# Two mixture-of-experts layers: blocks of 256 rows become units of 128, and the second layer goes by pairs of experts

## What is computed

```python
def _L0_ffn_ref(x, Wg, W1, b1, W2, b2):
    gate_logits = xs @ Wg
    weights, sel = jax.lax.top_k(gate_logits, TOP_K)
    weights = jax.nn.softmax(weights.astype(jnp.float32), axis=1).astype(x.dtype)
    h = jax.nn.relu(jnp.einsum('td,edf->etf', xs, W1) + b1[:, None, :])
    out_e = jnp.einsum('etf,efd->etd', h, W2) + b2[:, None, :]
    picked = out_e[sel, tok[:, None]]
    out = jnp.einsum('tk,tkd->td', weights, picked)
...
x = x + _L0_attn_a_ref(_layernorm(x, axis=-1), ...)
x = x + _L0_ffn_ref(_layernorm(x, axis=-1), L0_ffn_Wg, L0_ffn_W1, L0_ffn_b1, L0_ffn_W2, L0_ffn_b2)
x = x + _L0_attn_b_ref(_layernorm(x, axis=-1), ...)
x = x + _L0_ffn_ref(_layernorm(x, axis=-1), L0_ffn_Wg, L0_ffn_W1, L0_ffn_b1, L0_ffn_W2, L0_ffn_b2)
```

## Time and profile before

| | us |
|---|---|
| median of 3 runs | 2342.39 (2342.32 to 2342.47) |
| the profiled execution | 2342.5 |
| its span | 2340.8 |
| scan | 0 to 695 |
| ffn1: groups, routing, one-hots, block loop | 710.0, 758.5, 780.3, 838.8 to 1090.0 |
| attention | 1090 to 1757 |
| ffn2: one-hots, block loop, gather | 1850, 1908, 2157 to 2341 |

### The profile page before, as it was taken

How to read it: one execution, slowest core, us unless ns; L and a number is a source line. 1 busy time by engine, 2 the same in 40 slices (tenths; PEclk the granted TensorE clock), 3 DMA queues, 4 the chain that set the end, 5 groups by cost and what they waited for, 6 DMA issues and landing times. The chain is left out here.

```text
span 2340.8 us, 52167 instructions
## 1 busy us (share of the span) xinstructions
PE 1654.0 (71%) x16780; PEld 1352.2 (58%) x16780; DVE 1857.7 (79%) x4943; ACT 1471.0 (63%) x3849; POOL 1342.9 (57%) x1496
## 2 busy tenths in 40 slices
PE   4676675766657369995689999999986459998000
PEld 2444454454546158884488888888875338887000
DVE  6999999999978957776689999999975867776221
ACT  5666676766743647774388888888883457776000
POOL 3545555555540045554399999999971035553774
PEclk8778787777865679998699999999995579999555
DMA  1000001010034013333122222222214013333232
GB/s 29 14 14 22 20 14 28 14 27 14 19 104 140 1 48 81 81 80 58 39 57 57 57 59 59 59 57 57 57 28 129 23 27 81 81 81 67 74 80 57
DMA packets 188967, 122.59 MB, mean 52 GB/s; under 512 B 24320, under 2 KB 177824, under 8 KB 188704
## 3 DMA queue, kind: packets, MB, share of 16 engines
q1 hardware_dynamic: 154016, 75.18, 11.6%
q0 software_dynamic: 17408, 35.69, 6.9%
q10 hardware_dynamic: 17280, 8.40, 1.2%
HBM read 66.22 MB, written 44.04 MB: 47 GB/s over the span
## 5 line engine op out<-in xcount | busy, mean ns | idle before, releaser
L1044 POOL DMA_INDIRECT ffn_xs<-normed,ffn_tokeni x288 | 273.1, 948 | 460.1 <-DVE posi L1420 260.7
L1877 POOL TENSOR_TENSOR att_pl<-att_p,att_ph 128x384 f16<-128x384 f32 x512 | 455.3, 918 | 56.3 <-ACT att_ph L2098 48.6
L323 POOL TENSOR_TENSOR sq<-states,qS 128x256 f32<-128x256 f32 x256 | 250.9, 980 | 304.3 <-DVE states L733 303.3
L543 ACT ACTIVATE decayed<-states,alpha 128x64 f32<-128x64 f32 x1024 | 272.3, 336 | 177.6 <-DVE states L733 175.7
L379 PE MATMUL bank<-sq,ident 128*128 128x128 f32 x1024 | 249.9, 415 | 93.4 <-POOL sq L323 93.4
L2206 DVE TENSOR_REDUCE att_mx<-bank 128x3 f32<-128x384 f32 x512 | 279.9, 552 | 41.0 <-PE bank L1934 36.8
L1251 ACT ACTIVATE ffn_h<-bank,b_cols 128x256 f32<-128x256 f32 x576 | 226.4, 475 | 127.7 <-PE bank L1139 117.4
L379 PEld LDWEIGHTS bank<-sq,ident 128*128 128x128 f32 x1024 | 220.0, 240 | 128.9 <-POOL sq L323 100.7
L2095 ACT ACTIVATE att_p<-bank 128x384 f32<-128x384 f32 x512 | 252.2, 493 | 58.9 <-PE bank L1971 55.5
L2098 ACT ACTIVATE att_ph<-bank 128x384 f16<-128x384 f32 x512 | 253.0, 494 | 0.0
L1152 PE MATMUL bank<-w_h,ffn_hh 128*128 x1152 | 225.6, 223 | 14.9 <-DVE ffn_hl L1439 4.5
(11 more groups left out here) (336 smaller groups left out, 5085.5 us busy)
## 6 DMA issues: line engine op xcount, KB each, us to landing
slots<-ffn_ys SPq DMA_DIRECT2D x144, 128.0 KB
ffn_x_all<-x SPq DMA_DIRECT2D x16, 512.0 KB, 4.8
normed<-ffn_xn ACTq DMA_DIRECT2D x32, 256.0 KB, 2.3
att_qz<-att_qp SPq DMA_DIRECT2D x256, 32.0 KB
ffn_xs<-normed,ffn_tokeni POOLq DMA_INDIRECT x288
xin<-in_x SPq DMA_DIRECT2D x64, 64.0 KB, 2.0
xres<-in_x SPq DMA_DIRECT2D x64, 64.0 KB, 2.0
x<-x SPq DMA_DIRECT2D x64, 64.0 KB, 1.8
```

The costliest lines, as they stand in the source:

```text
L323: nc.gpsimd.tensor_tensor(sq[:, t, :].rearrange("p (h i j) -> p h i j", h=HL, i=D), states[:, t, :].rearrange("p (h i j) -> p h i j", h=HL ...
L543: ins = nc.scalar.activation(decayed[:, 64 * h:64 * h + 64], states[:, (t - 1) % TC, 64 * h:64 * h + 64], ACT.Copy, scale=alpha[p][:, t, h ...
L1044: pool.indirect_dma_start(xs[j % AHEAD][:, r, :], None, A["normed"], bass.IndirectOffsetOnAxis(ap=tokeni[:, BR * j + r:BR * j + r + 1], ax ...
L1877: nc.gpsimd.tensor_tensor(pl[:, h % RP, :], p32[:, h % RP, :], ph[:, h % RP, :], ALU.subtract).then_inc(low_done, 1)
```

## The change

The list of tokens is made in units of 128 rows (P) in place of blocks of 256, and `Layout` says how: ONE, for ffn1, has 8 groups and both choices (135 units); TWO, for ffn2, has 28 groups, one for each pair of experts, and each token once (91 blocks, each worked through by both of its experts: 182 units).

The normed rows are stored as two 16-bit halves; `turn` is two 16-bit matmuls (L1175) of halves already split. The first bias becomes row 127 of W1 (row 127 itself is subtracted from the rest; the normed rows sum to zero, and their last column is replaced by 1). W1 is therefore loaded as 127 rows (L814) and the bias as one (L815), and `last_row` (L837, 127 rows) is a copy of row 127 for all partitions, loaded between the first and the second part of x. The low parts of the weights, and the subtraction, go to GpSimd. ReLU goes from PSUM straight to the 16-bit high half; DVE forms the low half from PSUM.

In ffn2 a fetched row carries halves, x and both gates (1032 bytes, from `table`); DVE adds the first expert's result to x and then the second's, and GpSimd writes the finished 128 rows to `out` with one indirect transfer for each block (L1105). The gather stage is gone. The Python loops are unrolled.

```diff
-BS = 256
-BR = BS // P
-NB = 2 * NT // BR + NX
-NS = NB * BS
...
+XB = 8
+XH = 3
+HB = 4
+YB = 4
...
+class Layout:
+    def __init__(self, groups, choices):
+        self.groups, self.choices = groups, choices
+        self.blocks = (choices * B * T + groups * (P - 1)) // P
+        self.per = 3 - choices
+        self.units = self.blocks * self.per
+        self.listed = -(-self.units // AHEAD) * AHEAD
+ONE = Layout(NX, 2)
+TWO = Layout(PAIRS, 1)
+NS = ONE.blocks * P
...
+        w1 = self.A["W1"].rearrange("e d f -> d e f")
+        sp.dma_start(self.w[0][0:P - 1, :, :], w1[0:P - 1]).then_inc(self.w_in[0], 16)
+        sp.dma_start(self.w[0][P - 1:P, :, :], self.A["b1"].rearrange("(o e) f -> o e f", o=1)).then_inc(self.w_in[0], 16)
...
+        sp.wait_ge(self.cleared, 1)
+        sp.dma_start(self.last_row[0:P - 1, :, :], A["W1"][:, P - 1, :].partition_broadcast(P - 1)).then_inc(self.last_in, 16)
         sp.dma_start(X.b2[:, :, :].rearrange("p e d -> p (e d)"),
...
+                     A["b2"].rearrange("e d -> (e d)").partition_broadcast(P)).then_inc(self.b2_in, 16)
...
+    def subtract_last(self, pool, e):
+        if e == 0:
+            pool.wait_ge(self.raw_in[0], 32)
+            pool.wait_ge(self.last_in, 16)
+        self.nc.gpsimd.tensor_tensor(self.raw[0][:, e, :], self.raw[0][:, e, :], self.last_row[:, e, :],
+                                     ALU.subtract).then_inc(self.less, 1)
...
+    def high(self, act, n):
+        k, e = (1, n) if n < NX else (0, n - NX)
+        if n == 0:
+            act.wait_ge(self.raw_in[1], 16)
+        if k == 0:
+            act.wait_ge(self.less, e + 1)
+        scale = 2.0 ** (SPLIT, DSPLIT)[k]
+        a = self.nc.scalar.activation
+        a(self.parts(k, e)[0], self.raw[k][:, e, :], ACT.Copy, scale=scale).then_inc(self.w_high, 1)
+        act.wait_ge(self.w_high, n + 1)
+        a(self.raw[k][:, e, :], self.raw[k][:, e, :], ACT.Copy, scale=scale).then_inc(self.w_full, 1)
+    def low(self, pool, n):
+        k, e = (1, n) if n < NX else (0, n - NX)
+        pool.wait_ge(self.w_full, n + 1)
+        hi, lo = self.parts(k, e)
+        self.nc.gpsimd.tensor_tensor(lo, self.raw[k][:, e, :], hi, ALU.subtract).then_inc(self.w_low, 1)
...
+                sp.dma_start(x_all[:, NT // parts * k:NT // parts * (k + 1), :], srct[k]).then_inc(x_part[k], 16)
+                if k == 0 and setup:
+                    setup.loads(sp)
...
+            for g in range(NG):
+                sp.wait_ge(lo_s, g + 1)
+                sp.dma_start(splitt[g], split[g % 2][:, :, :]).then_inc(xn_kept[g % 2], 16)
+            if two:
+                sp.wait_ge(route, R["gate_b"])
+                sp.dma_start(A["table"][:, GATE_AT:GATE_AT + 2].rearrange("(n p) k -> p n k", p=P),
+                             gate[:, :, :]).then_inc(gates_kept, 16)
...
+            for j in range(NB):
+                if two:
+                    pool.wait_ge(ys_s, PER * (j + 1))
+                    for i in range(j - YB if j == NT else j - 1, j) if j >= NT else ():
+                        pool.wait_ge(kept[i % YB], 16 * (i // YB + 1))
+                    pool.indirect_dma_start(outt, bass.IndirectOffsetOnAxis(ap=tokeni[:, j:j + 1], axis=0),
+                                            ys[j % YB][:, :], None).then_inc(kept[j % YB], 16)
+                elif j + XB < NB:
+                    pool.wait_ge(xT_ps, j + 1)
+                if j + XB < NB:
+                    fetch(j + XB)
...
+            def turn(j):
+                pe.wait_ge(fetched[j % XB], before[j % XB] + 16 * (j // XB + 1))
+                if j >= 2:
+                    pe.wait_ge(x_cp, j - 1)
+                x = xs[j % XB][:, 0:P].bitcast(F16) if two else xs[j % XB][:, :]
+                for n in range(2):
+                    ins = mm(bank[j % 2][:, P * n:P * n + P], x[:, P * n:P * n + P], ident16[:, :], start=True, stop=True)
                 ins.then_inc(xT_ps, 1)
...
+            def up(u):
+                j = u // PER
+                pe.wait_ge(x_cp, j + 1)
+                if u >= HB:
+                    pe.wait_ge(h_low, u - HB + 1)
+                e = expert(pe, regs, u)
                 for c in range(FC):
...
+                    for n, (w, x) in enumerate(((0, 0), (0, 1), (1, 0))):
+                        ins = mm(bank[2 + u % HB][:, P * c:P * c + P],
+                                 X.w1[w][:, bass.ds(e, 1), c, :].rearrange("p o d -> p (o d)"), xhl[j % XH][:, x, :],
+                                 start=(n == 0), stop=(n == 2))
+                ins.then_inc(h_ps, 1)
+            def down(u):
+                pe.wait_ge(h_low, u + 1)
+                if u >= 2:
+                    pe.wait_ge(ys_s, u - 1)
+                if u == 0 and two:
+                    pe.wait_ge(b2_low, 1)
+                e = expert(pe, regs, u)
+                y = bank[6 + u % 2][:, 0:P]
+                if two:
+                    mm(y, X.all16[:, :], b2hl[:, bass.ds(e, 1), :].rearrange("p o d -> p (o d)"), start=True, stop=False)
+                for c in range(FC):
+                    for n, (w, h) in enumerate(((0, hh), (0, hl), (1, hh))):
+                        ins = mm(y, h[u % HB][:, c, :], X.w2[w][:, bass.ds(e, 1), c, :].rearrange("p o d -> p (o d)"),
+                                 start=(c == 0 and n == 0 and not two), stop=(c == FC - 1 and n == 2))
                 ins.then_inc(y_ps, 1)
...
+            if setup:
+                pe.wait_ge(setup.w_low, 2 * NX)
+            load_experts(pe, regs, 0)
+            turn(0)
+            turn(1)
+            for u in range(U):
+                up(u)
+                if u % PER == 0 and u // PER + 2 < NB:
+                    turn(u // PER + 2)
+                if u >= 2:
+                    down(u - 2)
+                refill(pe, regs, u)
+            down(U - 2)
+            down(U - 1)
...
+            def relu(u):
+                act.wait_ge(h_ps, u + 1)
+                if u >= HB:
+                    act.wait_ge(y_ps, u - HB + 1)
+                a(hh[u % HB][:, :, :].rearrange("p c t -> p (c t)"), bank[2 + u % HB][:, :], ACT.Relu).then_inc(h_high, 1)
...
-            for g in range(0 if dst is None else NG):
-                dve.wait_ge(X.got[g % AHEAD], 32 * Q * (g // AHEAD + 1))
-                for k, w in enumerate((g1, g2)):
-                    if k == 1:
-                        dve.wait_ge(halved, g + 1)
-                    for q in range(Q):
-                        t = Q * g + q
-                        ins = v.scalar_tensor_tensor(x_all[:, t, :], yg[g % AHEAD][:, k, q, :], w[:, t:t + 1],
-                                                     x_all[:, t, :], ALU.mult, ALU.add)
-                    ins.then_inc((halved, added)[k], 1)
...
-        ffn(nc, ctx, A, experts, ident, bank, "ffn2", A["x3"], A["out"])
+        ffn(nc, ctx, A, experts, ident, heads.ident16, bank, "ffn2", TWO, A["table"])
...
+            def split_h(u):
+                dve.wait_ge(h_high, u + 1)
+                v.scalar_tensor_tensor(hl[u % HB][:, :, :].rearrange("p c t -> p (c t)"), bank[2 + u % HB][:, :], 0.0,
+                                       hh[u % HB][:, :, :].rearrange("p c t -> p (c t)"), ALU.max, ALU.subtract).then_inc(h_low, 1)
+            def rows(u):
+                dve.wait_ge(y_ps, u + 1)
+                y = bank[6 + u % 2][:, 0:P]
+                if two:
+                    j, k = u // 2, u % 2
+                    x = xs[j % XB]
+                    if k == 0:
+                        v.scalar_tensor_tensor(acc[j % 2][:, :], y, x[:, GATE_AT:GATE_AT + 1], x[:, X_AT:X_AT + P],
+                                               ALU.mult, ALU.add).then_inc(ys_s, 1)
+                    else:
+                        if j >= YB:
+                            dve.wait_ge(kept[j % YB], 16 * (j // YB))
+                        dve.wait_ge(ys_s, u)
+                        v.scalar_tensor_tensor(ys[j % YB][:, :], y, x[:, GATE_AT + 1:GATE_AT + 2], acc[j % 2][:, :],
+                                               ALU.mult, ALU.add).then_inc(ys_s, 1)
                 else:
...
+                    if u >= YB:
+                        dve.wait_ge(kept[u % YB], 16 * (u // YB))
+                    v.scalar_tensor_tensor(ys[u % YB][:, :], y, 2.0 ** (-SPLIT - DSPLIT),
+                                           X.b2[:, bass.ds(expert(dve, regs, u), 1), :].rearrange("p o d -> p (o d)"),
+                                           ALU.mult, ALU.add).then_inc(ys_s, 1)
```

More of the change, by code:

```diff
@@ L901, in ffn @@
         own = Semaphores(nc)
+        two = lay is TWO
+        G, K, NB, NA, PER, U = lay.groups, lay.choices, lay.blocks, lay.blocks, lay.per, lay.units
+        UT = K * NT
+        SUMW = 512 if K == 2 else 448
+        SUMS = G * NT // SUMW
         x_all = sb("x_all", [P, NT, E])
         xn = [sb(f"xn{p}", [P, Q, E]) for p in range(2)]
+        split = [sb(f"split{p}", [P, Q, 2 * E], F16) for p in range(2)]
         eps = sb("eps", [P, 1])
@@ L936, in ffn @@
```

(72 more changed lines are left out.)

743 lines of the change are left out of this document (328 added, 415 removed).

## The result

The changed kernel takes 2607.5 us (2604.5 to 2609.5, 4 runs) beside 2342.4 for the kernel before on the same chip: a ratio of 1.113 [1.111, 1.115]. The profiled execution's span is 2603.8 us, 263.0 more than before's. The forecast was 2586.

What follows compares the result with a forecast made beforehand. The prediction took TensorE's stream to bound both block loops, with register pairs exposed in units of 128 rows. Terms +63 +86 +4 +72 -6 +192 -167 = +244 on a span of 2340.8, plus 1.7, gave 2586 us; stated range 2425 to 2635.

Steps and rivals of the forecast that it cites:

- scan's end behind W1's 127 rows: End of the scan: last stores of x queue behind W1's 127 rows on one DMA engine, 758.6 for 695.4, +63 us.
- ffn1 up to the first unit: Front of ffn1: parts of x queue behind last_row's 127 rows, +86 us; weight splitting and routing after the groups, +4.
- ffn1 loop: First expert layer's loop: 135 units of 2.33 us plus 6 make 321 us against 249, +72.
- attention and ffn2's front: Ahead of ffn2's loop: fewer, narrower one-hot rounds -24 us, wider routing passes and lead rows +18; -6, give or take 6.
- ffn2 loop: Second expert layer's loop: 182 units of 2.38 us plus 8 make 441 us against 249, +192.
- the end: Last stage: gather and stores of 184 us go, last scatter, its landing and release leave 17 us; -167.
- The upper end: Bound taken for W1's 127-row load: all on a single engine at 20.6 GB/s, 101 us; the other bound was nothing.
- Unit period: Both unit loops: eight chunks with register pairs at 0.24 us, plus waits and expert loads; 2.33 us in ffn1, 2.38 in ffn2.
- the 3.33 us of the kernel before: Block loops before: the array needs 2.87 us of a 3.33 us block; the rest was read as exposed register pairs.
- Rival C: Unit loops: register pairs hidden, units at the array's 1.46 us; 2301 us with the stall (chance 0.08), 2152 without (0.04).
- Rival D: Unit loops: TensorE's granted clock falls because the array is busy 62% in place of 86%; chance 0.06.
- Rival B: W1 and last_row loads: the 127 rows are spread over engines, so +149 us go, 2437 us; chance 0.17.

## Why the prediction was right, and where its numbers were off

The mechanisms of the likeliest case came as forecast. By its steps, on the profiled executions (stage bounds from the first and last weight loads of `up` and `down` in each loop and from SyncE's timeline):

| step | forecast | measured |
|---|---|---|
| scan's end behind W1's 127 rows | +63 | +54 (695.4 to 749.45) |
| ffn1 up to the first unit | +90 | +81 |
| ffn1 loop | +72 | +89 |
| attention and ffn2's front | -6 | -7 |
| ffn2 loop | +192 | +214 |
| the end | -167 | -168 |
| sum | +244 | +263 |

The stall came 18 us short and the loops 39 us long. These errors have opposite signs, so the sum is nearer than its terms; that much is luck.

- **127 rows.** The upper end was right, which the trace before could not show. The runs show it: while 127 rows are under way, the DMA share of 0.06 to 0.07 is one engine in 16. Why 127 rows go to one is not shown; that work is dealt in equal shares was my estimate. Its size was 1.2 times too high: one engine moves 25 GB/s, and not the 20.6 that I took from 16 engines at once, so 2.08 MB take 83 us and not 101. Both errors of the stall, -9 and -9, are that. SyncE itself was also held, for 77.75 and 77.87 us; that this changed nothing here, since all that was queued had to wait anyway, is my estimate.
- **Unit period.** 2.46 and 2.53 us in the mean of the steady part, against 2.33 and 2.38; half of the units take no more than 2.37 and 2.44. The chunk with a pair was right, 0.237 us. Mis-sized was the remainder: pauses, most of them under 0.2 us, stand between the chunks, 0.10 to 0.11 us a unit in the mean, and no wait explains them (in the second loop the distance from chunk to chunk inside `up` and `down` is 0.237 us in the median and 0.250 in the mean; 85 of 1092 are over 0.287, and one is 1.2). Over 317 units that makes some 34 of the 39 us by which the forecast of the loops was short; the rest lies in their starts and ends.
- **What the 3.33 us of the kernel before are made of.** The reason given here is not borne out. I put the difference to 2.87 down to pairs in the open. On the second chip the same eight pairs leave the blocks at 2.87, and taking them away gains nothing; on the first, TensorE's signals come up to 2 us late, the sequencer loses its lead, and the pairs come into the open behind that. They were seen in the open there rightly, 0.24 apart, and so priced rightly; that they were the cause was only argued, and how much of the 0.46 us would go with them on the first chip no run shows. The sum did not hang on it, because a unit of 128 rows has no cover in either case.
- **Rival C** is out by the measured loops, but its idea was half right: without pairs the changed kernel, with its loads split (and a wrong expert's result), beats the kernel before on the first chip (0.970), though far from the array's rate. **Rival D** is out: the clock was 0.98 to 1.00 in the loops with TensorE's array at 60% duty. In the traces it stands at 1.00 or 0.50 (in the one-hot rounds of the kernel before 1.00 from 1862 to 1866 us and 0.50 from 1868 to 1872), and 0.73 is the mean of both; what a unit takes at 0.50 no run shows. **Rival B** is the kernel with both loads split, 2481 us where it was put at 2437; the difference is the loops' 39 us, and some 7 more of ffn1's groups waiting for transfers, less small gains elsewhere.

No experiment points to a version of this change that computes the right result and beats the kernel before. With the loads split, its second expert layer still ends 1293 us after the first layer's loop (813.8 to its first unit, 461.8 in the loop, 17.6 behind it), against 1253.5 before (820.8, 247.9, 184.8): 40 us more with the pairs of experts, beside 89 us more in the first layer's loop and 11 in front of it.

## What to carry to other kernels

Count what the sequencer does for each piece of array work, not only the array work: halving the rows of a block doubled the share of address instructions, and 0.24 us for three matmuls of 0.17 us set the pace. Before a transfer's shape is trimmed, look at its number of rows: 127 in place of 128 cost 51 us, and with 112 + 15 the scan's last stores were issued at 676.80, beside 675.32 with 128. A cause read off one trace holds for that trace; the same program ran 84 us faster on another chip, with the gaps that I had explained gone. And where the profile names a releaser that had long been done, look at when its signals came: here the rows of the matmuls stood in time, and their signals came up to 2 us late.
